# Picked tables in couples: one comparison and one one-hot buffer for two embedding tables in a DLRM tower

## The chip, the cores and the metric

The kernel runs on one core of one Trainium2 chip. Its time is device microseconds (us) of one launch. Before the change three runs gave 159.5, 155.69 and 159.24 us, with a median of 159.24 us. One more execution was recorded by the hardware profiler: it took 156.0 us, of which the span from the first instruction of the program to the last is 154.2 us.

## The reference

For 512 samples the kernel looks up one row of 128 floats in each of 26 embedding tables, adds the sample's `r_bottom_output` as a first feature, takes all 351 dot products of two different features, and sends these with `r_bottom_output` through three layers:

```python
e = jnp.stack([tbl_0[ids[:, 0]], ..., tbl_25[ids[:, 25]]], axis=1)
all_emb = jnp.concatenate([bottom_output[:, None, :], embeddings], axis=1)
gram = jnp.einsum('bfd,bgd->bfg', all_emb, all_emb)
z = gram[:, _TRIU_I, _TRIU_J]
h = jnp.concatenate([z, r_bottom_output], axis=1)
h = jnp.maximum(h @ W_top1 + b_top1, 0.0)
h = jnp.maximum(h @ W_top2 + b_top2, 0.0)
y = h @ W_top3
```

Twelve tables have 1000 rows. The other fourteen have 1250, 12500 or 125000.

## The kernel before

The work has two sources of rows. The twelve tables of 1000 rows are **picked**: a table is loaded whole into SBUF as 128 partitions by 8 places (`RPP`) of 128 floats, and the rows are selected by matmuls against one-hot matrices. The other fourteen tables are **gathered**: an indirect DMA on GpSimd (POOL) brings the 128 rows that one tile of 128 samples needs from one table, 14 gathers for each of four tiles, 56 in all, written by the loop at L168 to L177.

One picked table `i` goes like this. Its 512 ids lie on all partitions in `ids_wide`. VectorE (DVE) writes seven of the eight places of the one-hot buffer `onehot[i % 2]`, one comparison of 128x512 each (L200). ScalarE (ACT) writes the eighth in two steps: `distance` = |id - row| (L256) and relu(1 - 4 * distance) (L269). ACT rounds the table to its high part `table_hi` (L266), DVE subtracts to get the low part `table_lo` (L191), and TensorE (PE) does eight matmuls with the high part (L369) and eight with the low part (L378) into one PSUM bank of `pick_ps`. ACT copies this bank into `features` (`pick_out`, L274). Places are taken in the order 4, 5, 6, 7, 1, 2, 3, 0.

The order of each engine's work is written by hand, and the engines meet at counting semaphores. These matter here. DVE begins the one-hots of table `i` when the picks up to `i - 2` are done (`picked_done`, L198). ACT begins `table_hi` of `i` at the same count (L264), but in its queue that stands behind `pick_out(i - 2)`. PE begins pick `i` when `table_hi` of `i` and `pick_out(i - 2)` are there. SyncE (SP) loads `ids_wide` of `i` and then the table `i` (L141 to L145), and before the load of table `i` it waits until both parts of table `i - 3` exist.

Between the picks stand the **turns**: PE transposes the gathered rows of up to four tables (L391), and DVE or ACT copies them to `features` (L186). `AFTER_PICK` says after which pick each turn comes; turns (t, g) of tile t and group g stand behind picks 2, 3, 4, 5, 7, 8, 9, 10 and 11. A turn holds up the picks behind it until its gathers have landed. The gathers of tiles 2 and 3 write over the rows of tiles 0 and 1, and wait until the same group of that tile is turned (L171).

When all picks are done the **tail** follows: for each tile the products of all feature couples (L404), their transposition on DVE into `grams[t % 2]` (L218, L220), a gathering of bands on ACT (L287), transposes of these (L415) and three layers (L421, L442, L449). In this document the picks are numbered from 0, and "pick 7" is the sixteen matmuls of the eighth picked table.

## Time and profile before

| | |
|---|---|
| runs | 159.5, 155.69, 159.24 us; median 159.24 us |
| profiled execution | 156.0 us, span 154.2 us |
| PE matmul busy | 108.1 us, 70% of the span |
| PE weight load busy | 89.8 us, 58% |
| DVE busy | 66.4 us, 43% |
| ACT busy | 59.2 us, 38% |
| POOL busy | 71.8 us, 47% |
| granted TensorE clock, mean | 0.856 of full speed |

The profiled execution is 3.2 us below the median and 0.3 us above the fastest run. The busy shares are means over stages that differ a lot: DVE is nearly always at work in the first 35 us, and rarely at work in the last 60.

### The profile page before, as it was taken

Reading aid. Unit: us, or ns where it says so; the run is one execution under the profiler, and the core shown is the slowest. Engines: PE = TensorE matmul, PEld = TensorE weight load, DVE = VectorE, ACT = ScalarE, POOL = GpSimd, SP = SyncE. Lnnn points to the kernel's source line nnn. Section 1 sums busy time; section 2 is a strip of 40 time slices with the busy share of each in tenths; the row PEclk is TensorE's granted clock in tenths of the full one; section 3 lists DMA queues with packets and bytes.
Section 4 is the critical chain, followed back from the end, with each engine's and each line's share of the span. In section 5 each row is a group of like instructions: output and inputs, shape, how many; then the busy total and the mean of one; then the engine's idle time right before and its main releaser. Section 6 shows DMA issues by size and latency. Waiting matters only on the chain.

```text
span 154.2 us, 3455 instructions
## 1 busy us (share of the span) xinstructions
PE 108.1 (70%) x1512; PEld 89.8 (58%) x1512; DVE 66.4 (43%) x121; ACT 59.2 (38%) x90; POOL 71.8 (47%) x63
## 2 busy tenths in 40 slices
PE   7598999109996866809429601853799949965994
PEld 7475788008884645608227401742798948855892
DVE  6799999983465439063084003060503005012100
ACT  3576998900455234064080006320304224300612
POOL 1479888997777877787787744000000000000000
PEclk9999999955999786996975865598579999997899
DMA  4999677467126397111112110000000000000000
GB/s 74 347 377 311 227 234 241 165 221 255 51 49 240 96 342 248 51 51 38 51 51 51 51 51 17 21 4 4 4 0 0 4 4 4 0 4 4 0 4 1
DMA packets 7089, 15.23 MB, mean 99 GB/s; under 512 B 1825, under 2 KB 2337, under 8 KB 7074
## 3 DMA queue, kind: packets, MB, share of 16 engines
q1 hardware_dynamic: 5138, 11.07, 20.8%
q0 software_dynamic: 1792, 3.67, 8.6%
q10 hardware_dynamic: 144, 0.26, 0.9%
q8 instruction: 12, 0.20, 0.6%
q14 instruction: 3, 0.02, 0.0%
HBM read 15.00 MB, written 0.00 MB: 97 GB/s over the span
## 4 chain that ended last, share of the span: by engine, by line
PE 35%; another core or an unknown queue 19%; issue 12%; POOL 11%; DMA 8%; ACT 8%; DVE 6%; ACTq 0%; DVEq 0%
POOL rows L174 11%; PE mlp_ps L421 10%; PE prod_ps L404 7%; DMA rows<-in_tbl_dram,ids_all 5%; PE mlp_ps L442 5%; PE mlp_ps L369 4%; PE mlp_ps L378 3%; DVE onehot L200 3%; PE turn_ps L391 3%; DMA ids_all<-in_ids_dram 3%; ACT features L186 2%; ACT table_hi L266 2%; ACT distance L256 1%; PE turn_ps L415 1%
## 5 line engine op out<-in xcount | busy, mean ns | idle before, releaser
L174 POOL DMA_INDIRECT rows<-in_tbl_dram,ids_all x56 | 71.1, 1269 | 23.6 <-issue 16.5
L200 DVE TENSOR_SCALAR onehot<-ids_wide,row_of 128x512 fp32r<-128x512 int32 x84 | 34.5, 485 | 24.4 <-remote 14.9
L369 PE MATMUL mlp_ps<-onehot,table_hi 128*128 128x512 f32 x96 | 31.7, 482 | 15.8 <-DVE onehot L200 13.1
L369 PEld LDWEIGHTS mlp_ps<-onehot,table_hi 128*128 128x128 f32 x96 | 21.6, 236 | 22.2 <-issue 15.5
L274 ACT COPY features<-mlp_ps 128x512 f32<-128x512 f32 x12 | 14.5, 1208 | 46.3 <-remote 28.2
L378 PE MATMUL mlp_ps<-onehot,table_lo 128*128 128x512 f32 x96 | 26.5, 422 | 0.4 <-DVE table_lo L191 0.4
L378 PEld LDWEIGHTS mlp_ps<-onehot,table_lo 128*128 128x128 f32 x96 | 19.7, 208 | 6.1 <-DVE table_lo L191 1.2
L391 PE MATMUL turn_ps<-ident,rows 128*128 128x128 f32 x56 | 10.2, 301 | 15.1 <-ACT features L186 7.2
L186 DVE COPY features<-turn_ps 128x512 f32<-128x512 f32 (+1 forms) x9 | 9.5, 1055 | 24.5 <-PE turn_ps L391 13.2
L404 PE MATMUL prod_ps<-features 128*27 128x27 f32 x1024 | 11.4, 203 | 11.3 <-issue 10.6
L404 PEld LDWEIGHTS prod_ps<-features 128*27 128x27 f32 x1024 | 10.5, 116 | 12.8 <-issue 11.8
L391 PEld LDWEIGHTS turn_ps<-ident,rows 128*128 128x128 f32 x56 | 7.5, 155 | 17.0 <-issue 8.6
L218 DVE STREAM_TRANSPOSE grams<-prod_ps 128x832 f32<-128x832 f32 x4 | 4.2, 1050 | 25.1 <-PE prod_ps L404 25.1
L191 DVE TENSOR_TENSOR table_lo<-table_raw,table_hi 128x1024 fp32r<-128x1024 f32 (+1 forms) x13 | 14.7, 1137 | 0.0
L266 ACT CAST table_hi<-table_raw 128x1024 fp32r<-128x1024 f32 (+1 forms) x12 | 12.1, 1008 | 0.3 <-DMA table_raw<-in_picked_dram 0.2
L421 PE MATMUL mlp_ps<-pairs,w_sb 128*128 128x128 f32 x96 | 11.9, 282 | 0.0
L421 PEld LDWEIGHTS mlp_ps<-pairs,w_sb 128*128 128x128 f32 x96 | 11.6, 200 | 0.0
L287 ACT COPY bands<-grams 128x117 f32<-128x117 f32 (+1 forms) x8 | 3.9, 497 | 16.3 <-DVE grams L218 16.1
L256 ACT ACTIVATE distance<-ids_wide,minus_row 128x512 f32<-128x512 int32 x12 | 8.6, 713 | 2.8 <-DMA ids_wide<-in_picked_ids_dram 2.7
L442 PE MATMUL mlp_ps<-h,w_sb 128*128 128x128 f32 x64 | 9.5, 307 | 0.0
L442 PEld LDWEIGHTS mlp_ps<-h,w_sb 128*128 128x128 f32 x64 | 8.8, 218 | 0.3 <-ACT h L292 0.2
L186 ACT COPY features<-turn_ps 128x512 f32<-128x512 f32 (+1 forms) x7 | 7.4, 1060 | 2.7 <-remote 1.9
(30 smaller groups left out, 52.4 us busy)
## 6 DMA issues: line engine op xcount, KB each, us to landing
table_raw<-in_picked_dram SPq DMA_DIRECT2D x11, 512.0 KB
ids_wide<-in_picked_ids_dram SPq DMA_DIRECT2D x11, 256.0 KB, 3.9
w_sb<-in_W_top_dram SPq DMA_DIRECT2D x4, 256.0 KB
rows<-in_tbl_dram,ids_all POOLq DMA_INDIRECT x56
table_raw<-in_picked_dram SPq DMA_DIRECT2D x2, 256.0 KB, 4.8
w_sb<-in_W_top_dram SPq DMA_DIRECT2D x1, 512.0 KB
ids_wide<-in_picked_ids_dram ACTq DMA_DIRECT2D x1, 256.0 KB, 4.6
bottom_t<-in_bottom_turned_dram SPq DMA_DIRECT2D x1, 256.0 KB
```

Of the source, the lines that this page charges most:

```text
L174: nc.gpsimd.indirect_dma_start(out=rows[t % 2][:, slot - FIRST_G, :], out_offset=None, in_=tables[table], in_offset=bass.IndirectOffsetOnA ...
L186: return engine_copy(dst, turn_ps[n % 2][:, 0:len(slots), :])
L191: return nc.vector.tensor_tensor(table_lo[i % 2][:, begin:end, :], table_raw[i % RAWS][:, begin:end, :], table_hi[i % 2][:, begin:end, :]. ...
L200: nc.vector.tensor_scalar(onehot[i % 2][:, c, :], ids_wide[:, i, :], row_of[:, c:c + 1], None, ALU.is_equal).then_inc(onehot_ready, 1)
L266: nc.scalar.copy(table_hi[i % 2][:, 0:end, :], table_raw[i % RAWS][:, 0:end, :]).then_inc(hi_ready, 1)
L274: nc.scalar.copy(features[:, :, 1 + i], pick_ps[i % 2][:].rearrange("p a b -> p (a b)")).then_inc(picks_ready, 1)
L369: nc.tensor.matmul(acc, table_hi[i % 2][:, c, :], onehot[i % 2][:, c, :], start=(n == 0), stop=False)
L378: last = nc.tensor.matmul(acc, table_lo[i % 2][:, c, :], onehot[i % 2][:, c, :], start=False, stop=(n == RPP - 1))
L391: last = nc.tensor.transpose(turn_ps[n % 2][:, i, :], rows[t % 2][:, slot - FIRST_G, :], ident[:])
L404: last = nc.tensor.matmul(prod_ps[t % 2][32 * s:32 * s + FEATURES, m, 0:FEATURES], features[:, b, :], features[:, b, :], start=True, stop= ...
L421: return nc.tensor.matmul(mlp_ps[n // 2][:, n % 2, :], w1_sb[:, c, 128 * n:128 * n + 128], rhs, start=start, stop=stop, skip_group_check=True)
L442: last = nc.tensor.matmul(mlp_ps[m][:, 2, :], w2_sb[:, c, 128 * m:128 * m + 128], h1[:, c, :], start=(c == 0), stop=(c == 3))
```

## The change

Picked tables go in couples `j` of tables `2j` and `2j + 1`. `ids_wide` becomes two buffers of 2 x 512 ids, loaded alternately, with two semaphores where there were twelve. Each `onehot` buffer holds 8 places x 2 x 512. One DVE comparison covers 1024 ids: six times seven comparisons of 128x1024 stand where twelve times seven of 128x512 stood. ACT's `distance` and its relu also cover 1024 ids, six of each. The table's high and low parts, the sixteen matmuls, `pick_out` and all gathers are as before, one for each table.

The waits shift with it. DVE begins the one-hots of couple `j` when picks up to `2j - 3` are done, and its wait for pick `i - 2` now stands ahead of `table_lo` of each table. ACT writes the eighth place of a couple behind the same count. SP loads the ids of couple `j` ahead of table `2j - 1`, and before that waits until the one-hots of couple `j - 2` are complete. `grams` has one buffer where it had two, so DVE's transposition of tile `t` also waits for ACT's bands of tile `t - 1`.

```diff
-        ids_wide = sb("ids_wide", [128, PICKS, BATCH], i32)
+        ids_wide = [sb(f"ids_wide{i}", [128, 2, BATCH], i32) for i in range(2)]
-        onehot = [sb(f"onehot{i}", [128, RPP, BATCH], f32r) for i in range(2)]
+        onehot = [sb(f"onehot{i}", [128, RPP, 2, BATCH], f32r) for i in range(2)]
-        grams = [sb(f"grams{i}", [128, FEATURES - 1 + BANDS, SLOTS]) for i in range(2)]
+        grams = sb("grams", [128, FEATURES - 1 + BANDS, SLOTS])
@@ sync
-                sp.dma_start(ids_wide[:, i, :], picked_ids[i].partition_broadcast(128)).then_inc(wide_in[i], 16)
+                if i % 2 == 1 and i + 1 < PICKS:
+                    j = (i + 1) // 2
+                    if j >= 2:
+                        sp.wait_ge(onehot_ready, (RPP - ACT_RPP) * (j - 1))
+                        sp.wait_ge(distance_ready, ACT_RPP * (j - 1))
+                    sp.dma_start(ids_wide[j % 2][:], picked_ids[j].partition_broadcast(128)).then_inc(wide_in[j % 2], 16)
@@ vector, pick_operands(i)
-                dve.wait_ge(wide_in[i], 16)
-                if i >= 2:
-                    dve.wait_ge(picked_done, i - 1)
-                for c in PLACES[:-ACT_RPP]:
-                    nc.vector.tensor_scalar(onehot[i % 2][:, c, :], ids_wide[:, i, :], row_of[:, c:c + 1],
-                                            None, ALU.is_equal).then_inc(onehot_ready, 1)
+                if i % 2 == 0:
+                    j = i // 2
+                    dve.wait_ge(wide_in[j % 2], 16 * (j // 2 + 1))
+                    if j >= 2:
+                        dve.wait_ge(picked_done, 2 * (j - 1))
+                    for c in PLACES[:-ACT_RPP]:
+                        nc.vector.tensor_scalar(onehot[j % 2][:, c, :, :], ids_wide[j % 2][:], row_of[:, c:c + 1],
+                                                None, ALU.is_equal).then_inc(onehot_ready, 1)
...
+                if i >= 2:
+                    dve.wait_ge(picked_done, i - 1)
                 low_half(i, 0, HALF if i == 0 else RPP).then_inc(lo_ready, 1)
@@ vector, grams_out(t)
+                if t >= 1:
+                    dve.wait_ge(bands_ready, 2 * t)
@@ scalar, table_high(i): distance and the relu only for even i, on [:, c, :, :]
+                    if j >= 2:
+                        act.wait_ge(picked_done, 2 * (j - 1))
@@ scalar, first load
-            act.dma_start(ids_wide[:, 0, :], picked_ids[0].partition_broadcast(128)).then_inc(wide_in[0], 16)
+            act.dma_start(ids_wide[0][:], picked_ids[0].partition_broadcast(128)).then_inc(wide_in[0], 16)
@@ tensor, pick(i)
-                        pe.wait_ge(onehot_ready, (RPP - ACT_RPP) * i + n + 1)
-                    nc.tensor.matmul(acc, table_hi[i % 2][:, c, :], onehot[i % 2][:, c, :],
+                        pe.wait_ge(onehot_ready, (RPP - ACT_RPP) * (i // 2) + n + 1)
+                    nc.tensor.matmul(acc, table_hi[i % 2][:, c, :], onehot[i // 2 % 2][:, c, i % 2, :],
```

## Rows read from the trace of the kernel before

**Rows 1.** Busy time by stretch: length, then each engine's busy us, clock, DMA, GB/s.

```profile
0.00:34.60 34.60, 24.60 (x108) 19.11 (x108) 31.52 (x64) 23.89 (x31) 25.93 (x20) 0.95 0.73 245
34.60:95.60 61.00, 38.65 (x136) 30.20 (x137) 24.71 (x44) 19.22 (x25) 45.26 (x44) 0.78 0.35 106
95.60:154.20 58.60, 44.81 (x1268) 40.52 (x1268) 10.18 (x13) 16.10 (x35) 0.66 (x1) 0.88 0.02 5
```

**Rows 2.** Timeline, the turn behind pick 4: start, us, engine, what, idle before it.

```profile
25.76 1.99 PE L378 MATMUL mlp_ps<-onehot,table_lo 128*128 128x512 f32 x8
34.62 1.12 PE L391 MATMUL turn_ps<-ident,rows 128*128 128x128 f32 x4 [6.88 <-DMA rows<-in_tbl_dram,ids_all]
```

**Rows 3.** Timeline of POOL, four of its 56 gathers (6th, 12th, 29th, 54th).

```profile
13.03 3.31 POOL L174 DMA_INDIRECT rows<-in_tbl_dram,ids_all  x1 [0.30 <-issue]
...
26.30 6.70 POOL L174 DMA_INDIRECT rows<-in_tbl_dram,ids_all  x1 [0.30 <-issue]
...
56.88 1.18 POOL L174 DMA_INDIRECT rows<-in_tbl_dram,ids_all  x1 [0.31 <-issue]
...
90.18 0.95 POOL L174 DMA_INDIRECT rows<-in_tbl_dram,ids_all  x1 [0.30 <-issue]
```

**Rows 4.** All gathers: ns shortest/median/longest, first and last start in us.

```profile
L174 POOL DMA_INDIRECT rows<-in_tbl_dram,ids_all x56: 940/960/6702, 5.8 to 95.3; - x56
```

**Rows 5.** Waits in total: engine, what, waited for, us, times, longest.

```profile
ACT features L274 <- remote: 28.2, 4, 13.2
```

**Rows 6.** Timeline around pick 10: its last matmuls, its turn, those who wait.

```profile
72.69 2.01 PE L378 MATMUL mlp_ps<-onehot,table_lo 128*128 128x512 f32 x8
74.54 0.38 PE L391 MATMUL turn_ps<-ident,rows 128*128 128x128 f32 x2
...
93.78 1.17 ACT L274 COPY features<-mlp_ps 128x512 f32<-128x512 f32 x1 [13.24 <-remote]
94.06 0.94 POOL L174 DMA_INDIRECT rows<-in_tbl_dram,ids_all  x1 [2.94 <-remote]
```

**Rows 7.** Timeline of one slow round, from pick 7's copy to pick 9's start.

```profile
56.59 1.17 ACT L274 COPY features<-mlp_ps 128x512 f32<-128x512 f32 x1 [5.54 <-PE mlp_ps L378]
56.67 2.86 DVE L200 TENSOR_SCALAR onehot<-ids_wide,row_of 128x512 fp32r<-128x512 int32 x7 [4.65 <-PE mlp_ps L378]
58.14 1.04 ACT L266 CAST table_hi<-table_raw 128x1024 fp32r<-128x1024 f32 x1
59.23 3.47 PE L369 MATMUL mlp_ps<-onehot,table_hi 128*128 128x512 f32 x8 [2.69 <-issue]
```

**Rows 8.** Groups by shape: line, engine, operation, count, busy us, mean ns, idle before.

```profile
L191 DVE TENSOR_TENSOR table_lo<-table_raw,table_hi 128x1024 fp32r<-128x1024 f32 x11 | 13.4, 1221 | 0.0
L191 DVE TENSOR_TENSOR table_lo<-table_raw,table_hi 128x512 fp32r<-128x512 f32 x2 | 1.3, 678 | 0.0
L266 ACT CAST table_hi<-table_raw 128x1024 fp32r<-128x1024 f32 x11 | 11.5, 1044 | 0.2 <-DMA table_raw<-in_picked_dram 0.2
L266 ACT CAST table_hi<-table_raw 128x512 fp32r<-128x512 f32 x1 | 0.6, 622 | 0.1
L256 ACT ACTIVATE distance<-ids_wide,minus_row 128x512 f32<-128x512 int32 x12 | 8.6, 713 | 2.8 <-DMA ids_wide<-in_picked_ids_dram 2.7
L269 ACT ACTIVATE onehot<-distance 128x512 fp32r<-128x512 f32 x12 | 7.6, 634 | 0.0
```

**Rows 9.** Timeline of the start: first comparisons, pick 0's last matmuls.

```profile
5.41 2.86 DVE L200 TENSOR_SCALAR onehot<-ids_wide,row_of 128x512 fp32r<-128x512 int32 x7 [1.02 <-DMA ids_wide<-in_picked_ids_dram]
...
8.93 2.11 PE L378 MATMUL mlp_ps<-onehot,table_lo 128*128 128x512 f32 x8
```

**Rows 10.** Timeline of the tail: bands of tile 0, transposition of tile 1.

```profile
102.81 1.02 ACT L287 COPY bands<-grams 128x117 f32<-128x117 f32 x2 [4.88 <-DVE grams L218]
...
109.54 1.05 DVE L218 STREAM_TRANSPOSE grams<-prod_ps 128x832 f32<-128x832 f32 x1 [5.29 <-PE prod_ps L404]
```

**Rows 11.** Timeline of DVE, the batch of comparisons before the 12th gather's end.

```profile
30.00 2.88 DVE L200 TENSOR_SCALAR onehot<-ids_wide,row_of 128x512 fp32r<-128x512 int32 x7
```

More of the change, by code:

```diff
@@ L65, in dlrm_tower @@
         minus_row = sb("minus_row", [128, RPP])
-        distance = sb("distance", [128, ACT_RPP, BATCH])
+        distance = sb("distance", [128, ACT_RPP, 2, BATCH])
         table_raw = [sb(f"table_raw{i}", [128, RPP, DIM]) for i in range(RAWS)]
@@ L94, in dlrm_tower @@
         ids_in = sem("ids_in")
-        wide_in = [sem(f"wide_in{i}") for i in range(PICKS)]
+        wide_in = [sem(f"wide_in{i}") for i in range(2)]
         first_half_in = sem("first_half_in")
@@ L249, in table_high @@
             def table_high(i):
-                act.wait_ge(wide_in[i], 16)
-                if i >= 1:
-                    act.wait_ge(onehot_act, ACT_RPP * i)
-                for c in range(ACT_RPP):
-                    nc.scalar.activation(distance[:, c, :], ids_wide[:, i, :], ACT.Abs, bias=minus_row[:, c:c + 1]
+                j = i // 2
+                if i % 2 == 0:
+                    act.wait_ge(wide_in[j % 2], 16 * (j // 2 + 1))
+                    if j >= 1:
+                        act.wait_ge(onehot_act, ACT_RPP * j)
+                for c in range(ACT_RPP if i % 2 == 0 else 0):
+                    nc.scalar.activation(distance[:, c, :, :], ids_wide[j % 2][:], ACT.Abs, bias=minus_row[:, c:c + 1]
                                          ).then_inc(distance_ready, 1)
@@ L266, in table_high @@
                 nc.scalar.copy(table_hi[i % 2][:, 0:end, :], table_raw[i % RAWS][:, 0:end, :]).then_inc(hi_ready, 1)
-                for c in range(ACT_RPP):
-                    act.wait_ge(distance_ready, ACT_RPP * i + c + 1)
-                    nc.scalar.activation(onehot[i % 2][:, c, :], distance[:, c, :], ACT.Relu, bias=1.0, scale=-4.0
+                for c in range(ACT_RPP if i % 2 == 0 else 0):
+                    act.wait_ge(distance_ready, ACT_RPP * j + c + 1)
+                    if j >= 2:
+                        act.wait_ge(picked_done, 2 * (j - 1))
+                    nc.scalar.activation(onehot[j % 2][:, c, :, :], distance[:, c, :, :], ACT.Relu, bias=1.0, scale=-4.0
                                          ).then_inc(onehot_act, 1)
@@ L281, in bands_out @@
             def bands_out(t):
-                gram = grams[t % 2][:]
+                gram = grams[:]
                 for half, (begin, end) in enumerate(((0, 1), (1, CHUNKS))):
@@ L377, in pick @@
                         pe.wait_ge(lo_ready, 1)
-                    last = nc.tensor.matmul(acc, table_lo[i % 2][:, c, :], onehot[i % 2][:, c, :],
+                    last = nc.tensor.matmul(acc, table_lo[i % 2][:, c, :], onehot[i // 2 % 2][:, c, i % 2, :],
                                             start=False, stop=(n == RPP - 1))
@@ L508 @@
     ids = _np.asarray(inputs["ids"])
-    arrays["picked_ids"] = _np.ascontiguousarray(ids[:, PICKED].T)
+    arrays["picked_ids"] = _np.ascontiguousarray(ids[:, PICKED].T).reshape(COUPLES, 2, BATCH)
     picked = _np.zeros((PICKS, 128 * RPP, DIM), _np.float32)
```

7 lines of the change are left out of this document (4 added, 3 removed).

## The prediction, made before the changed kernel was built

> **What bounds the kernel now.** I read the share table by stretch first, because one mean for the span hides three stages [rows 1]. In the first 34.6 us DVE is busy 31.5 us: this is the stage in which the change removes work. In the next 61.0 us no engine is busy all the time: PE 38.7, DVE 24.7, ACT 19.2, POOL 45.3. The last 58.6 us is the tail, in which POOL is idle but for one gather and DVE works 10.2 us. So the time is the end of the picks (about 95.6 us) plus the tail (58.6 us) plus 1.8 us that lie outside the span, together 156.0 us. The tail's matmuls are not touched. The question is what moves the 95.6 us.
>
> The timeline of PE names the first limit. Pick 4 ends at 27.75, and the turn behind it starts at 34.62: PE sat still for 6.9 us until gathered rows had landed [rows 2]. The rows are those of the twelfth gather, which POOL began at 26.30 and held for 6.70 us [rows 3]. The reader is to see that DVE's 31.5 us, though nearly all of the stage, are not what PE waits for at its end.
>
> The second limit is odd, and the argument has to live with it. The list of waits has ACT's copy of the picks waiting 28.2 us in four stretches for "remote", that is for an increment whose sender the trace can't name [rows 5]. The code names it: it is PE's own `picked_done`. Pick 10 shows its last matmul ending at 74.70 and its turn at 74.92; ACT starts the copy of pick 10 at 93.78, and POOL, which waits for that turn before its 55th gather, goes on at 94.06 [rows 6]. Two engines see PE's increments 19 us late, at the same time. So PE's increments arrive late in this stage, and no row says why. What the rows do say is when: the lateness is there while POOL issues one gather after another, the median 0.96 us long with 0.30 us between [rows 4], and it is gone 2.6 us after the 54th gather ended at 91.13 [rows 3]. I take it as a working assumption that the late increments belong to this stream of gathers, and that the stage ends soon after POOL runs out of gathers that it may issue.
>
> **The change part by part.** *DVE's comparisons.* Seven of 128x512 take 2.86 us [rows 7], 0.41 us each from start to start. No row shows this operation at 1024. The subtraction on the same engine has both widths, 678 and 1221 ns: 543 ns for 512 more columns, so 135 ns are fixed [rows 8]. With 135 ns fixed, a comparison of 1024 takes 2 x 0.41 - 0.135 = 0.68 us. The bounds are 0.82 us, if nothing is fixed, and 0.62 us, if as much is fixed as on ACT, where a cast goes from 622 to 1044 ns and so has 200 ns fixed [rows 8]. A batch of seven is then 4.8 us (4.3 to 5.7) for two tables, where two batches took 5.7: 0.9 us saved per couple, 5.7 us in all (0 to 8.4). About half lies in the first 34.6 us.
>
> *ACT.* By the slope of the cast (422 ns for 512 columns), `distance` goes from 713 to 1135 ns and the relu from 634 to 1056 ns, six of each instead of twelve [rows 8]. That saves 6 x (0.29 + 0.21) = 3.0 us of ACT in all. In order of work it cuts both ways: `table_hi` of an even table stands behind a `distance` that is 0.42 us longer, that of an odd table comes 0.71 us earlier. ACT's `pick_out`, then `distance`, then `table_hi` lead straight to the next pick but one: 56.59 to 59.18, and PE starts pick 9 at 59.23 [rows 7]. So this chain of 2.6 us gets 0.15 us shorter on the mean of an even and an odd table, 1 us over the seven picks behind 34.6 us. I count it at nothing, because by the assumption above POOL's stream and not this chain sets the end of the stage; if the chain set it, 1 us would be gained.
>
> *The start.* The first ids are 512 KB where they were 256 KB, and the first comparison could start at 5.41 [rows 9]. I allow 0 to 1.4 us for the extra 256 KB and take 0.9, since at the 245 GB/s of the stage [rows 1] 256 KB take 1.1 us and share with the loads of the table. Then the batch ends at 6.3 + 4.8 = 11.1, against 8.27, and pick 0, which ended at 11.04 [rows 9], ends at about 13.7. The second couple follows the low parts of tables 0 and 1, so by then the delay is 1.9 us, and it stays there, since from pick 1 on PE's own work (about 4.1 us for each pick with its turn) is as long as DVE's: 2.4 us of comparisons, 1.2 of subtraction and half a turn's copy. Pick 4 would end at 29.6 instead of 27.75. This costs nothing while the turn behind pick 4 waits for its rows until 34.6; if the rows come early, 1.9 us are lost.
>
> *SP's queue.* The ids of couple 2 wait for couple 0's one-hots, and tables 3 and later are queued behind that wait. Table 3 is held anyway until the low part of table 0 exists, which DVE writes just behind those one-hots, so the wait adds nothing. All table loads of the start move by 1.9 us with the low parts, as do their users.
>
> *Wider gates.* DVE begins couple `j` when pick `2j - 3` is done, one pick earlier than the even table needed before. In the late stage, where DVE waited for increments, that takes DVE's 2.9 us out of the line; but PE started at the end of `table_hi`, before DVE had finished [rows 7], so nothing is gained: ACT's chain is next, and it is as late as before.
>
> *One `grams` buffer.* The added wait is for bands that ACT finished at 103.83, and DVE comes to need the buffer at 109.54 [rows 10]: 5.7 us of cover, and as much again in the later tiles. Cost nothing; queued behind it on DVE is a turn's copy that PE needs 20 us later.
>
> *POOL.* This is where the sum is decided. The gathers themselves are unchanged, but POOL's share of time with DVE at work is not. In DVE's busy stage the 6th gather took 3.31 us and the 12th 6.70 us [rows 3]; the median of all is 0.96 [rows 4]. The 12th ended at 33.00, just behind DVE's batch of 30.00 to 32.88 [rows 11], having seen a batch, a subtraction and a batch go by. Yet the 29th took 1.18 us from 56.88, in the middle of the batch of 56.67 to 59.53 [rows 7]. So a batch holds a gather by chance and until the batch's end. After the change there are six batches of 4.8 us for twelve of 2.86: DVE's busy total shrinks by 5.7 us, each hold is up to 1.9 us longer, and there are half as many. Twelve gathers cost 33.0 - 5.8 = 27.2 us [rows 3, 4] against 15 at the free pace of 0.96 + 0.30 = 1.26; the 12.2 us of holds become anything from 6 (no double hold) to 15 us. I take 11, with DVE's total: a gain of 1 us.
>
> The Trainium skill (SBUF — State Buffer, "Who interferes with whom") states that a DVE instruction in a two-port mode and GpSimd block each other for the whole instruction, the later one waiting in full, and (same page, "SBUF: two separate sides") that descriptors of GpSimd's DMAs can't be written meanwhile. By that rule comparisons of 0.68 us hold each gather longer than those of 0.41, which speaks against the change. The 12th gather agrees (6.70 us), the 29th (1.18 us inside a batch) shows that the hold ends between two instructions at times. By the rule in full the holds would come out at their upper end of 15 us, 3 us more than now, and the sum at 156 + 3 = 159 us; by the rows it is 155.
>
> *Sum.* 156.0 - 1 (POOL) - 0 (ACT's chain) + 0 (start, hidden) + 0 (`grams`) = 155 us on the profiled execution's scale. That execution lay 3.2 us under the median of the three runs, of which one is near it and two are at 159. I expect the changed kernel to scatter alike, and give 155 + 3 = 158 us.
>
> **The rivals.** *Faster: the double hold of the twelfth gather goes.* If the batches leave POOL a gap there, the twelfth gather takes 1.7 us instead of 6.7, so PE's 6.9 us of waiting shrink by 5, less 1.9 if pick 4 ends later; POOL's stream, on which I hang the end of the stage, is 5 us earlier: 156 - 5 = 151, or 154 with the median's offset of 3. For it: DVE has less work and starts couples with more lead. Against: DVE still has 19 us of comparisons for the first four couples without a pause. Chance 0.33.
>
> *Slower: longer holds.* The place is again the first 35 us. A gather that is caught across a batch, two subtractions, a turn's copy and another batch waits 4.8 + 2.4 + 1.2 + 4.8 = 13.2 us instead of 6.7, and the first turns then wait for gathers already behind pick 3. This costs up to 6.5 us: 156 + 6.5 + 3 = 165 us at most, and 163 for two thirds of it. It decides as soon as one gather meets DVE without a pause through two batches. The same ending comes if the comparison at 1024 ran at half the rate (1.2 us each, 8.5 a batch): DVE would take 5.4 us a table and pick 4 would end 5 us later. Chance 0.22 together. The Trainium skill's rule of full blocking (the same section) would lead here too.
>
> *The late increments go.* If they belong not to the gathers but to DVE's and ACT's waits for each table, coupling could end them. Picks 6 to 11 would follow each other in 5 us instead of 10, the products would start when the rows of turn (2, 2) land near 75, and the time would be 156 - 20 = 136 us, 139 on the median's scale. Nothing in the rows points there. Chance 0.05.
>
> *The change does little of what it says* is contained in the forecast: DVE's saving is real but not on the path. Forecast 0.40.
>
> **How the numbers follow.** A run-to-run scatter of 3.8 us in the three runs means that about 2%, or 3.2 us, is what this kernel's measurement can tell from no change. The forecast's own range is 155 to 161. Faster by over 2% (under 156.1) takes the faster rival and the last one, 0.38 together. Slower by over 2% (over 162.4) is the slower rival's but for a hundredth: 0.21. The rest, 0.41, lies within. The range from 150 to 163.5 holds the forecast, the faster rival and the milder half of the slower one, and leaves out 0.05 below and about 0.1 above.
>
> **What would show it.** Comparisons of 128x1024 at 0.68 us from start to start; pick 0's end near 13.7; 42 comparisons with some 29 us busy; ACT's copies of picks 6 to 10 still waiting for "remote"; the 54th gather ending between 85 and 93, and products starting some 4 us later; a tail of 58 to 59 us. The prediction is wrong if the products start far from 2 to 6 us behind POOL's last unheld gather, since then the late increments don't hang on the gathers, and wrong in sign if the twelfth gather's landing moves by more than 5 us either way.

## The result and the profile after

The changed kernel took 148.11 us in the median of four runs (144.81 to 150.53), the kernel before 157.47 us in four runs beside it. The ratio is 0.938, with a 95% interval from 0.928 to 0.948. It is faster by 6%, and 148.11 us lies below the predicted range (150 to 163.5). A ratio here compares only the faster executions of the two kernels, of the kernel before often no more than two or three, which leaves a verdict at the 2% mark open for the experiments up to e15; the medians beside it are of all executions. Its profiled execution took 144.81 us, of which the span is 143.0 us.

By stretch (the same view as [rows 1]; the second stretch ends where the products start at full rate):

```profile
0.00:34.60 34.60, 31.87 (x131) 25.54 (x132) 29.54 (x42) 24.01 (x25) 23.30 (x28) 1.00 0.79 257
34.60:86.00 51.40, 27.29 (x148) 20.62 (x146) 21.07 (x25) 18.69 (x19) 36.78 (x36) 0.79 0.39 120
86.00:143.00 57.00, 43.19 (x1236) 38.80 (x1235) 10.53 (x14) 15.22 (x34) 0.00 (x0) 0.86 0.01 3
```

The tail is 57.0 us where it was 58.6. What went is in front of it: 86.0 us for 95.6. POOL has done 28 pieces of work by 34.6 us where it had done 20; 7 of these are start-up work in both, so 21 gathers stand for 13. None is left for the tail. Why the tail is 1.6 us shorter, no run was made to tell.

The groups of gathers, comparisons and the other parts that the prediction costed:

```profile
L180 POOL DMA_INDIRECT rows<-in_tbl_dram,ids_all x56 | 59.3, 1059 | 21.2 <-issue 16.8 <-DMA ids_all<-in_ids_dram 4.4
L208 DVE TENSOR_SCALAR onehot<-ids_wide,row_of 128x1024 fp32r<-128x1024 int32 x42 | 28.6, 750 | 1.2 <-DMA ids_wide<-in_picked_ids_dram 1.2
...
L197 DVE TENSOR_TENSOR table_lo<-table_raw,table_hi 128x1024 fp32r<-128x1024 f32 x11 | 13.4, 1222 | 4.9 <-issue 4.6
L280 ACT CAST table_hi<-table_raw 128x1024 fp32r<-128x1024 f32 x11 | 11.9, 1078 | 0.9 <-DMA table_raw<-in_picked_dram 0.9
```

POOL's busy time in the gathers is 59.3 us, mean 1059 ns, though no gather was touched. The same line in the trace of before has 11.8 us more:

```profile
L174 POOL DMA_INDIRECT rows<-in_tbl_dram,ids_all x56 | 71.1, 1269 | 23.6 <-issue 16.5 <-DMA ids_all<-in_ids_dram 4.2 <-remote 2.9
```

The timeline of the changed kernel's gathers, from the fourth gather to the twelfth and the last, shows why:

```profile
10.28 1.02 POOL L180 DMA_INDIRECT rows<-in_tbl_dram,ids_all  x1 [0.30 <-issue]
11.60 0.94 POOL L180 DMA_INDIRECT rows<-in_tbl_dram,ids_all  x1 [0.30 <-issue]
...
14.10 1.02 POOL L180 DMA_INDIRECT rows<-in_tbl_dram,ids_all  x1 [0.30 <-issue]
15.42 1.02 POOL L180 DMA_INDIRECT rows<-in_tbl_dram,ids_all  x1 [0.30 <-issue]
16.75 1.02 POOL L180 DMA_INDIRECT rows<-in_tbl_dram,ids_all  x1 [0.30 <-issue]
...
21.26 1.88 POOL L180 DMA_INDIRECT rows<-in_tbl_dram,ids_all  x1 [0.30 <-issue]
...
81.11 0.94 POOL L180 DMA_INDIRECT rows<-in_tbl_dram,ids_all  x1 [0.30 <-issue]
```

The free pace is 0.95 us and 0.30 us between; inside DVE's batches most gathers take 1.02 us, and the longest of the twelve takes 1.88 us. DVE's second batch, seven comparisons in 4.84 us, from 12.78 to 17.62, covers three of them whole and most of a fourth:

```profile
5.61 4.87 DVE L208 TENSOR_SCALAR onehot<-ids_wide,row_of 128x1024 fp32r<-128x1024 int32 x7 [1.23 <-DMA ids_wide<-in_picked_ids_dram]
...
12.78 4.84 DVE L208 TENSOR_SCALAR onehot<-ids_wide,row_of 128x1024 fp32r<-128x1024 int32 x7
```

The twelfth gather ends at 23.14; it ended at 33.00 [rows 3]. The 56th ends at 82.05; before, already the 54th ended at 91.13. On PE, the turn behind pick 4 follows without a wait (before: 6.88 us, [rows 2]), and the picks run on until the last turns. Then comes what was late before too:

```profile
28.33 1.99 PE L394 MATMUL mlp_ps<-onehot,table_lo 128*128 128x512 f32 x8
30.16 0.60 PE L407 MATMUL turn_ps<-ident,rows 128*128 128x128 f32 x4
...
60.83 1.03 PE L407 MATMUL turn_ps<-ident,rows 128*128 128x128 f32 x8
78.14 0.50 PE L420 MATMUL prod_ps<-features 128*27 128x27 f32 x24 [16.27 <-issue]
80.25 0.20 PE L420 MATMUL prod_ps<-features 128*27 128x27 f32 x1 [1.61 <-issue]
83.04 0.20 PE L420 MATMUL prod_ps<-features 128*27 128x27 f32 x1 [2.60 <-issue]
...
86.55 2.50 PE L420 MATMUL prod_ps<-features 128*27 128x27 f32 x190 [0.46 <-issue]
```

PE is through with pick 11 at 61.0 and with the last turns at 61.9. By the code its products wait for ACT's copy of pick 11, and that copy waits for PE's own increment (`picked_done`), seen 16 us late as in [rows 5, 6]:

```profile
76.76 1.17 ACT L290 COPY features<-mlp_ps 128x512 f32<-128x512 f32 x1 [16.24 <-remote]
```

The copy ends at 77.93 and the products begin at 78.14, but then they come singly, and PE is at full rate only 4.5 us after the last gather.

### The profile page after: what moved, and what is told of

Same layout as the page of the kernel before. It is cut to its first block, busy times and chain, and to the rows that moved or that the text cites. A ratio compares the mean times of both kernels' runs of the same rounds, so it can differ in the third digit from the quotient of the medians.

```text
span 143.0 us, 3394 instructions
## 1 busy us (share of the span) xinstructions
PE 102.3 (72%) x1512; PEld 85.0 (59%) x1512; DVE 61.1 (43%) x79; ACT 57.9 (40%) x78; POOL 60.1 (42%) x63
## 4 chain that ended last, share of the span: by engine, by line
PE 64%; issue 25%; DMA 3%; ACT 3%; DVE 2%; DVEq 0%; ACTq 0%
PE mlp_ps L385 18%; PE mlp_ps L394 16%; PE mlp_ps L437 11%; PE prod_ps L420 9%; PE turn_ps L407 5%; DMA ids_wide<-in_picked_ids_dram 3%; PE mlp_ps L458 3%; PE turn_ps L431 2%; DVE grams L230 1%; PE mlp_ps L465 1%; ACT bands L303 1%; ACT features L192 1%; ACT distance L270 1%; DVE features L192 0%; ACT table_hi L274 0%
## 5 line engine op out<-in xcount | busy, mean ns | idle before, releaser
L180 POOL DMA_INDIRECT rows<-in_tbl_dram,ids_all x56 | 59.3, 1059 | 21.2 <-issue 16.8
L420 PE MATMUL prod_ps<-features 128*27 128x27 f32 x1024 | 13.5, 210 | 33.9 <-issue 33.1
L420 PEld LDWEIGHTS prod_ps<-features 128*27 128x27 f32 x1024 | 11.7, 123 | 36.1 <-issue 35.1
L385 PE MATMUL mlp_ps<-onehot,table_hi 128*128 128x512 f32 x96 | 27.6, 429 | 2.7 <-ACT table_hi L274 1.6
L208 DVE TENSOR_SCALAR onehot<-ids_wide,row_of 128x1024 fp32r<-128x1024 int32 x42 | 28.6, 750 | 1.2 <-DMA ids_wide<-in_picked_ids_dram 1.2
L394 PE MATMUL mlp_ps<-onehot,table_lo 128*128 128x512 f32 x96 | 25.0, 404 | 0.4 <-issue 0.4
L385 PEld LDWEIGHTS mlp_ps<-onehot,table_hi 128*128 128x128 f32 x96 | 18.0, 198 | 8.8 <-issue 2.9
L192 ACT COPY features<-turn_ps 128x512 f32<-128x512 f32 (+1 forms) x7 | 7.4, 1059 | 9.4 <-remote 8.9
L458 PE MATMUL mlp_ps<-h,w_sb 128*128 128x128 f32 x64 | 8.3, 280 | 0.0
L308 ACT ACTIVATE h<-mlp_ps 128x256 f32<-128x256 f32 x8 | 3.1, 384 | 12.4 <-PE mlp_ps L437 12.4
L270 ACT ACTIVATE distance<-ids_wide,minus_row 128x1024 f32<-128x1024 int32 x6 | 6.9, 1144 | 2.9 <-DMA ids_wide<-in_picked_ids_dram 2.9
```

Of the source, the lines that this page charges most:

```text
L180: nc.gpsimd.indirect_dma_start(out=rows[t % 2][:, slot - FIRST_G, :], out_offset=None, in_=tables[table], in_offset=bass.IndirectOffsetOnA ...
L192: return engine_copy(dst, turn_ps[n % 2][:, 0:len(slots), :])
L208: nc.vector.tensor_scalar(onehot[j % 2][:, c, :, :], ids_wide[j % 2][:], row_of[:, c:c + 1], None, ALU.is_equal).then_inc(onehot_ready, 1)
L385: nc.tensor.matmul(acc, table_hi[i % 2][:, c, :], onehot[i // 2 % 2][:, c, i % 2, :], start=(n == 0), stop=False)
L394: last = nc.tensor.matmul(acc, table_lo[i % 2][:, c, :], onehot[i // 2 % 2][:, c, i % 2, :], start=False, stop=(n == RPP - 1))
L420: last = nc.tensor.matmul(prod_ps[t % 2][32 * s:32 * s + FEATURES, m, 0:FEATURES], features[:, b, :], features[:, b, :], start=True, stop= ...
```

## The experiments

Two things had to be settled: what let the gathers through (wider comparisons, or the couples' structure and loads), and whether POOL's last gather really sets the end of the stage. Kernels that ran together share a chip, and their ratios are to the kernel before on that chip.

### The comparison's width: e1_narrow, e2_ids_couples

e1 is the changed kernel with each comparison split by table (calls shortened):

```diff
-  tensor_scalar(onehot[j % 2][:, c, :, :], ids_wide[j % 2][:], row_of[:, c:c + 1], None, ALU.is_equal)
+  tensor_scalar(onehot[j % 2][:, c, 0, :], ids_wide[j % 2][:, 0, :], row_of[:, c:c + 1], None, ALU.is_equal)
+  tensor_scalar(onehot[j % 2][:, c, 1, :], ids_wide[j % 2][:, 1, :], row_of[:, c:c + 1], None, ALU.is_equal)
```

> The changed kernel with each comparison of 128x1024 split into two of 128x512, with everything else (couples, buffers, waits, counts) as changed. Theory 1, the width: the comparisons of 1024 let POOL's gathers through where those of 512 held them; then long gathers come back (one of over 3 us among the first twelve), the twelfth ends near 33 us instead of 23, and the time is that of the kernel before, 155 to 159 us. Rival, the structure: what counts is that DVE and ACT get work a table earlier; then the gathers stay short and the time stays at 145 to 150 us, with some 6 us more of DVE busy time hidden.

Measured: 164.55 us beside 161.46, ratio 1.040 (1.023 to 1.057). The holds are back, and worse than the kernel before's; the twelfth gather ends at 40.21, where theory 1 had 33:

```profile
11.53 7.58 POOL L180 DMA_INDIRECT rows<-in_tbl_dram,ids_all  x1 [0.30 <-issue]
...
24.45 4.45 POOL L180 DMA_INDIRECT rows<-in_tbl_dram,ids_all  x1 [0.30 <-issue]
...
31.03 6.67 POOL L180 DMA_INDIRECT rows<-in_tbl_dram,ids_all  x1 [0.30 <-issue]
```

e2 is the kernel before with its ids loaded by couples (the waits of DVE and ACT for the ids follow, not shown):

```diff
-  sp.dma_start(ids_wide[:, i, :], picked_ids[i].partition_broadcast(128)).then_inc(wide_in[i], 16)
+  if i % 2 == 1 and i + 1 < PICKS:
+      sp.dma_start(ids_wide[:, i + 1:i + 3, :], picked_ids[(i + 1) // 2].partition_broadcast(128)
+                   ).then_inc(wide_in[i + 1], 16)
```

> The kernel before, with its ids loaded for two tables at a time: six transfers of 512 KB instead of twelve of 256 KB; comparisons and waits as before. Rival, the transfers: if the smaller number of transfers frees the gathers, the twelfth gather ends near 23 us and the time falls to about 148 us. Theory 1 (the width) and the structure both expect no change: 155 to 159 us, the twelfth gather near 33 us.

Measured: 160.59 us (158.07 to 163.88) beside 161.46: no difference that can be told, and the twelfth gather ends at 33.20. Everything of the change but the width of the comparison loses 2% by the medians, 4% by the ratio; the loads alone do nothing. So the width is the gain. The changed kernel itself did not run beside these two; e7 and e8 below make the same comparison side by side.

### Columns or pattern: e7_flat, e8_wide256

e7 writes the comparison of the changed kernel as one row of 1024 columns; e8 splits it the other way, 256 ids of both tables in each (512 columns in two rows; calls shortened):

```diff
+  # e7
+  tensor_scalar(onehot[j % 2][:, c, :, :].rearrange("p a b -> p (a b)"),
+                ids_wide[j % 2][:].rearrange("p a b -> p (a b)"), row_of[:, c:c + 1], None, ALU.is_equal)
+  # e8, for k in 0, 1
+  tensor_scalar(onehot[j % 2][:, c, :, 256 * k:256 * k + 256],
+                ids_wide[j % 2][:, :, 256 * k:256 * k + 256], row_of[:, c:c + 1], None, ALU.is_equal)
```

> The changed kernel with the same comparisons written over one run of 1024 ids instead of two of 512. If the number of columns of one instruction lets the gathers through, nothing changes: gathers of 1.0 us among DVE's comparisons, 145 to 150 us. Rival: the pattern of two rows does it, and then gathers of over 3 us come back and the time is above 155 us.

> The changed kernel with each comparison split in two, but across: each half covers 256 ids of both tables, so it has 512 columns in two rows. If the number of columns decides, it behaves like the split by table: long gathers, 160 to 166 us. If the pattern of two rows decides, it behaves like the change: 145 to 150 us.

Measured: e7 119.55 us, ratio 0.935 (0.910 to 0.959), longest gather 1.88 us; e8 131.53 us, ratio 1.028 (1.011 to 1.046), longest gather 4.05 us:

```profile
53.39 4.05 POOL L180 DMA_INDIRECT rows<-in_tbl_dram,ids_all  x1 [0.30 <-issue]
```

The number of columns in one instruction decides, not how they lie: e8 is 10% slower than e7, which ran beside it. The times expected for both (145 to 150 and 160 to 166 us) were missed, for a reason of the session: during these runs, on one chip, the kernel before took 129.5 us; in all others its median is 157 to 162 us. The ratio of the change is the same. More of that below.

### Why 512 columns hold a gather: e11_drained, e13_wide_drained

A comparison of 512 columns is 479 ns long in the records, but a batch of seven takes 2.86 us, 0.41 us each: they overlap. Those of 1024 columns overlap as much, 750 ns long and 0.68 us from start to start. And the overlapping narrow ones do not hold every gather: in the first two batches of the kernel before (from 5.41 and 9.40) four gathers took 1.10 to 1.25 us; the 3.31 us of [rows 3] came with the third. In e11, the kernel before, each waits for the signal of the one before it; e13 does the same to the changed kernel.

```diff
-  for c in PLACES[:-ACT_RPP]:
+  for k, c in enumerate(PLACES[:-ACT_RPP]):
+      if k:
+          dve.wait_ge(onehot_ready, (RPP - ACT_RPP) * i + k)      # e13: j for i
```

> The kernel before, in which each comparison of 128x512 also waits for the signal of the one before it, so that they don't overlap: a start to start of about 0.55 us in place of 0.40 and a batch of 3.9 us in place of 2.9. If it is the gapless succession of short comparisons that holds a gather, the gaps let gathers through, no gather takes over 2.5 us, the 12th ends before 28 us and the time falls by 3 to 6% below the kernel before, in spite of the longer batches. If a comparison of 512 columns holds gathers whatever the gap, holds of 3 to 7 us stay, or grow with the batch, and the time is that of the kernel before or 1 to 2% above.

> A version that may beat both kernels: the changed kernel in which each comparison of 128x1024 also waits for the signal of the one before it. If gaps between comparisons let gathers through whatever the width, most gathers take 0.95 us in place of 1.02 to 1.28, POOL's busy time falls from 59 to 54 to 56 us, and the last gather ends 3 to 5 us earlier than in the changed kernel, near 78. Where full-rate products start 4.0 to 4.5 us after the last gather, the time is then 2 to 3% below the changed kernel's. The other theory: a batch of seven takes 5.4 us in place of 4.8, DVE comes later, and PE waits for one-hots, so that the time is the changed kernel's or up to 2% above.

Measured for e11: 150.21 us (145.3 to 151.29) beside 158.07 (154.09 to 162.82, seven runs), 5% less with no overlap of the two; an interval isn't given for it. DVE's batches grew from 2.86 to 4.21 us, the comparisons keep DVE busy for 46.4 us where it was 34.5 (e12), and the kernel is faster. The first batch and the gathers in it:

```profile
5.18 4.21 DVE L202 TENSOR_SCALAR onehot<-ids_wide,row_of 128x512 fp32r<-128x512 int32 x7 [0.79 <-DMA ids_wide<-in_picked_ids_dram]
```

```profile
6.95 0.95 POOL L174 DMA_INDIRECT rows<-in_tbl_dram,ids_all  x1 [0.30 <-issue]
8.20 0.95 POOL L174 DMA_INDIRECT rows<-in_tbl_dram,ids_all  x1 [0.30 <-issue]
```

No gather takes over 1.89 us, and the twelfth ends at 21.99. So comparisons of 512 columns do not hold a gather as such; those 0.41 us from start to start can, those 0.60 us apart did not. Whether it is the overlap or the closer succession that matters, the runs do not part: the 1024-column comparisons overlap too and hold nothing.

Measured for e13: 148.51 us, ratio 0.934 (0.921 to 0.946), against 0.917 (0.909 to 0.926) for the changed kernel beside it. It gains nothing over the changed kernel, and my expectation fails: the gathers keep POOL busy for 64.7 us where I had 54 to 56, and the last one ends at 87.22 where I had 78. In a batch a gather takes 1.27 us, 1.58 us from start to start:

```profile
16.02 1.27 POOL L180 DMA_INDIRECT rows<-in_tbl_dram,ids_all  x1 [0.30 <-issue]
17.60 1.28 POOL L180 DMA_INDIRECT rows<-in_tbl_dram,ids_all  x1 [0.30 <-issue]
```

Its comparisons start every 5.53 / 7 = 0.79 us, and 1.58 is two of these. In the changed kernel gathers start every 1.33 us (15.42, 16.75) with comparisons every 0.67 to 0.69 us: two again. In e11 two comparisons take 1.20 us, less than a gather's own 1.25, and nothing is held. The rows fit a GpSimd that gets through one gather for every two comparisons, so that slower comparisons, once nothing is held, only cost. This was not tested otherwise, and it does not explain the holds: two comparisons 0.41 us apart take 0.82 us, less than 1.25. Why gathers are held there stays open.

### Early or late holds: e9_narrow_early, e10_narrow_late, e12_before

e9 splits as e1 does for couples 0 to 2 (`if j < 3`), e10 for couples 3 to 5 (`if j >= 3`); e12 is the kernel before.

> The changed kernel with the comparisons of couples 0 to 2 split into two of 128x512, and those of couples 3 to 5 left at 1024 columns. If the gain is that the first 12 gathers land earlier for the first turns, nearly all of it goes: the 12th gather ends after 30 us, the turn behind pick 4 waits again, and the time is 3 to 5% above the changed kernel's. If it is the end of POOL's whole stream (late holds count as much as early ones), about half of the loss of the fully split kernel comes here, some 3 to 4 us.

> The mirror: couples 0 to 2 at 1024 columns, couples 3 to 5 split. By the first theory (early gathers feed the turns) this costs nothing, since the picks run ahead with rows to spare: within 1% of the changed kernel, if TensorE's signals are prompt on this chip. By the second theory it costs the other half, 3 to 4 us, and the last gather ends 3 to 5 us later than in the changed kernel.

> The kernel before as it is, for a trace on this chip beside the other three. Holds of 3 to 7 us by the batches of 512-column comparisons are expected on any chip. If TensorE's signals are prompt here, the span is near 128 us; if they are late, as in the first traces, it is 154 to 160 us. Both theories say the same of this run: it only tells which kind of chip the other three ran on.

Measured: e9 152.62 us, ratio 0.982 (0.964 to 1.000); e10 152.17 us, 0.967 (0.938 to 0.997); e12 155.93 us. Against the changed kernel's ratios on other chips (0.938 and 0.917) each half costs 3 to 7%; as the changed kernel did not run beside them and both intervals are wide, the halves can't be told apart. Late holds cost about as much as early ones, where the theory of the early gathers had them cost nothing: the last gather ends at 89.06 in e9 and 90.53 in e10. They make PE wait for rows too, three times in e10's trace (of the execution of 153.87 us), the longest before the turn that precedes the products:

```profile
67.12 1.12 PE L413 MATMUL turn_ps<-ident,rows 128*128 128x128 f32 x4 [4.33 <-DMA rows<-in_tbl_dram,ids_all]
```

But the products then still crawl until behind the last gather, so at this pace of the gathers it is the end of POOL's stream that counts. How the stage ends in e12:

```profile
68.53 0.66 PE L391 MATMUL turn_ps<-ident,rows 128*128 128x128 f32 x4 [3.17 <-DMA rows<-in_tbl_dram,ids_all]
69.12 0.69 PE L404 MATMUL prod_ps<-features 128*27 128x27 f32 x37
70.32 0.24 PE L404 MATMUL prod_ps<-features 128*27 128x27 f32 x1 [0.52 <-issue]
71.02 0.20 PE L404 MATMUL prod_ps<-features 128*27 128x27 f32 x1 [0.45 <-issue]
...
91.31 0.20 PE L404 MATMUL prod_ps<-features 128*27 128x27 f32 x1 [2.60 <-issue]
...
96.21 2.02 PE L404 MATMUL prod_ps<-features 128*27 128x27 f32 x152 [0.46 <-issue]
```

The picks are done at 64.9 and the products begin at 69.12, but after 37 of them they come singly, at steps of 0.70 us or a multiple, "issue" before each: PE waits for nothing that the trace shows. Full rate returns 4.3 us after the last gather. So in all traces of this kind (times read from the timelines, the products' first long group being full rate):

| us | last gather ends | products at full rate | span |
|---|---|---|---|
| after | 82.05 | 86.55 | 143.0 |
| e13 | 87.22 | 91.49 | 145.8 |
| e9 | 89.06 | 93.43 | 150.4 |
| e10 | 90.53 | 94.96 | 152.1 |
| e12 (before) | 91.92 | 96.21 | 154.1 |
| e2 | 98.75 | 102.88 | 158.4 |
| e1 | 102.46 | 106.50 | 162.8 |

4.0 to 4.5 us in every row. e12 also shows how much the holds differ between executions of one kernel: its twelfth gather ends at 28.94 and its longest takes 3.61 us, where the first trace of before had 33.00 and 6.70; the spans are 154.1 and 154.2 us all the same. In the first trace of before, in e11 and in e14 PE's increments were late during the picks instead, the picks ended only at 83 to 91, and the products' full rate came 0.4 to 2.8 us after the last gather. So e14's expectation (4.0 to 4.5 us behind the last gather, at 82 to 84 us) missed: POOL, too, waited for PE's increments there, and its last gather ended at 86.21.

### Fewer gathers: e3_before_half, e4_after_half

The kernels before and after with the gathers of tiles 2 and 3 left out (their turns read the rows of tiles 0 and 1; two waits change with it, not shown):

```diff
-  for t in range(TILES):
+  for t in range(2):
```

> The kernel before, without the gathers of tiles 2 and 3 (28 of 56 left; tiles 2 and 3 use the rows of tiles 0 and 1). Theory 2, the gathers make PE's increments late and their end sets the end of the stage: POOL is done near 52 us, from some 3 us later on no increment is late, picks follow each other in 5 us, and the products start near 75 us instead of 96: about 135 us. Rival, PE's increments are late for a reason of PE's own work: the late ones stay up to the last pick, the products start near 95 us and the time stays over 150 us.

> The changed kernel, without the gathers of tiles 2 and 3 (28 of 56 left; tiles 2 and 3 use the rows of tiles 0 and 1). Theory 2: POOL is done near 42 us, the last picks end near 60 us as now, but the products start right then, at 62 us instead of 86, so about 121 us. Rival (PE's own work makes them late): the copy of pick 11 still waits until about 76 us and the time stays near 145 us.

Measured: e3 128.21 us, ratio 0.813 (0.805 to 0.822), no wait for "remote" in its trace, products at 68.43, just behind the picks. e4 136.6 us (129.52 to 139.22) where 121 was expected; no ratio is given. The first bears the assumption out: without POOL's late gathers the stage ends with the picks. The second was a surprise. Its 28 gathers run unheld, one each 1.25 us, and are done at 42.26; by then PE had stood for 9.1 us. The trace is of an execution of 139.22 us and another took 129.52 us, so how much of this all four had isn't known:

```profile
26.22 0.38 PE L405 MATMUL turn_ps<-ident,rows 128*128 128x128 f32 x2
27.43 0.27 PE L405 MATMUL turn_ps<-ident,rows 128*128 128x128 f32 x1 [0.83 <-issue]
28.16 0.32 PE L405 MATMUL turn_ps<-ident,rows 128*128 128x128 f32 x1 [0.46 <-issue]
37.59 3.78 PE L383 MATMUL mlp_ps<-onehot,table_hi 128*128 128x512 f32 x8 [9.11 <-issue]
```

The picks' own matmuls come singly here between 43.65 and 45.05, and are at full rate from 45.75, 3.5 us after the last gather. The 33 us from there to the products at 78.72 are picks at 4 us each.

Where the holds are gone the early stretch may suffer: gathers in close succession seem to do harm that held ones do not. e14's trace, of an execution of 143.71 us in which no gather took over 2.0 us, has such a stretch as well (ACT's copy at 47.50 waited 14.45 us for "remote"). That is a theory on their pace.

### The pace of the gathers: e5 and e6, e14, e15 to e18

A memset on POOL and a wait for it stand ahead of each gather of tiles 1 to 3 of the changed kernel:

```diff
+  if t >= 1:                                            # e18: t >= 2
+      nc.gpsimd.memset(pause[:], 0.0).then_inc(paused, 1)
+      paused_times += 1
+      pool.wait_ge(paused, paused_times)
```

`pause` is 128x512 in e5, e15 and e18, 128x1024 in e6, 128x128 in e16 and 128x256 in e17.

> The changed kernel with a pause on POOL before each gather of tiles 1 to 3: a memset of 128x512 into a scratch tile, and a wait for it, some 0.6 us more per gather. Theory 2a, the density of the gathers makes PE's increments late: with one gather in about 1.9 us none is late, the products start near 62 us instead of 86, the tail is held a little by the gathers of tile 3 (the last near 105 us), and the time is 120 to 128 us. Rival 2b, gathers at any density do it until the last one is done: the gathers end near 105 us and the time is about 165 us.

> As the last one, with a memset of 128x1024, some 1.1 us more per gather, so one gather in about 2.4 us. Theory 2a: no late increments either, but tile 3's rows come near 122 us, so 132 to 140 us. Rival 2b: the end of the stage moves with the last gather, about 185 us. If 0.6 us is too short a pause and 1.1 is not, this one is faster than the last.

Measured, in the session of e7 and e8: e5 130.48 us, ratio 1.018 (1.003 to 1.033), e6 142.35 us, 1.116 (1.098 to 1.135). They told nothing of the theory, because no engine waited for "remote" there: e7's products start at full rate at 60.20, right behind the picks, though its gathers go on until 82.92.

```profile
59.61 0.66 PE L408 MATMUL turn_ps<-ident,rows 128*128 128x128 f32 x4 [0.53 <-DMA rows<-in_tbl_dram,ids_all]
60.20 3.46 PE L421 MATMUL prod_ps<-features 128*27 128x27 f32 x219
```

So e5 ran once more in a session in which the kernel before took 162.29 us, beside the changed kernel (e14). The memsets are not free for DVE: its comparisons are 889 ns long on the mean in e5 and 1042 ns in e6, for 748 in e7.

> The changed kernel as it is, beside the other two on this chip. On a chip where the kernel before takes 155 to 162 us, full-rate products should start 4.0 to 4.5 us after the last gather (82 to 84 us), and the time be 146 to 150 us; on one where the kernel before takes 129 us they start right behind the picks, near 60 us, and the time is 119 to 122 us. The ratio to the kernel before is 0.93 to 0.95 on both.

> The kernel e5 once more: a memset on POOL ahead of each gather of tiles 1 to 3, so that gathers come about every 3 us in place of 1.25 and the last one ends near 101 us. Where the kernel before takes 129 us it gives 130 us again and tells nothing new. Where it takes 155 to 162 us: if PE is served slowly as long as any gather is still to come, full-rate products start 4 us after the last gather, near 105, and the time is 162 to 165 us. If it is the close succession of gathers that does it, PE runs as on the other chip and the time is 129 to 135 us, below the changed kernel's 148.

Measured: e14 145.15 us, ratio 0.917 (0.909 to 0.926); e15 135.72 us, 0.856 (0.846 to 0.866). The last gather ends at 102.21, 16 us later than in e14, and the kernel is 6.5% faster: it is the pace. Gathers start 1.91 us apart among DVE's comparisons (not 3, as I had expected) and 1.76 us apart behind them, where the products are. PE gets some 42 products done in each of these intervals:

```profile
73.71 0.32 PE L427 MATMUL prod_ps<-features 128*27 128x27 f32 x5 [0.46 <-issue]
74.46 0.70 PE L427 MATMUL prod_ps<-features 128*27 128x27 f32 x37 [0.43 <-issue]
75.48 0.30 PE L427 MATMUL prod_ps<-features 128*27 128x27 f32 x4 [0.32 <-issue]
76.22 0.70 PE L427 MATMUL prod_ps<-features 128*27 128x27 f32 x38 [0.44 <-issue]
```

```profile
73.10 0.95 POOL L187 DMA_INDIRECT rows<-in_tbl_dram,ids_all  x1 [0.27 <-POOL pause L184]
74.86 0.95 POOL L187 DMA_INDIRECT rows<-in_tbl_dram,ids_all  x1 [0.27 <-POOL pause L184]
```

The last three ask how long the gap must be, and where.

> As e15 with the smallest pause: a memset of 128x128 and a wait ahead of each gather of tiles 1 to 3, so that gathers start about 1.5 us apart in place of 1.25 (and 1.91 in e15). If TensorE is freed in proportion to the gap between two gathers, products still come a few at a time until 4 us after the last gather (near 88), and the time is 142 to 148 us. If any gap behind a gather is enough, PE is served as in e15 and the rows come earlier than there: 128 to 133 us.

> The pause between the two: 128x256, gathers about 1.65 us apart, the last one ending near 93. By the first theory the time is between those of e16 and e15, or the best of the three if e15 pauses longer than it needs (133 to 140 us); by the second it is that of e16 plus up to 2 us.

> The pause of e15 (128x512) only ahead of the gathers of tiles 2 and 3; tiles 0 and 1 come at full pace, as in the changed kernel, until about 42 us. If it is the products' stretch behind the picks that must be free of a close succession, this is as good as e15 or better, 130 to 135 us. If the close succession in the first 40 us already sets off the late signals, as in e4, where half the gathers at full pace gave 137 us, the time is 137 to 145 us, with a stretch of over 8 us in which PE starts nothing.

Measured, beside 157.45 us for the kernel before: e16 146.6 us, ratio 0.929 (0.922 to 0.937); e17 141.08 us, 0.897 (0.890 to 0.905); e18 144.78 us, 0.903 (0.893 to 0.914). e12, e14 and e15 ran on other chips than these three.

| gathers start apart, in the products' stretch | products done per interval | ratio to before |
|---|---|---|
| 1.25 us (e12, e14) | 1 or 2 (e12) | 0.917 (e14) |
| 1.44 us (e16) | some 10 | 0.929 |
| 1.55 us (e17) | some 20 | 0.897 |
| 1.76 us (e15) | some 42 | 0.856 |

For the products the effect grows with the dose: the longer the gap, the more of them pass. From 1.25 to 1.76 us they grow by some 41 for 0.51 us, 80 for each us added (47 and 67 for the two smaller pauses); PE's long groups run at 76 (190 in 2.50 us, above) to 109 (239 in 2.19 us, e15's at 103.61) for each us. So, by this estimate, PE works at most at its full rate in the time that the pause adds, and hardly at all in the rest. The time follows only from 1.55 us on: at 1.44 us it is no better than without a pause (0.929 and 0.917). e18 has the long gap only from tile 2 on, and in its trace, of an execution of 146.54 us (the four took 141.27 to 147.4), PE stands for 8.4 us in the early stretch, as e4's did:

```profile
35.98 3.63 PE L392 MATMUL mlp_ps<-onehot,table_hi 128*128 128x512 f32 x8 [8.41 <-issue]
```

With its ratio of 0.903 against e15's 0.856 on another chip, this speaks for the early gathers' pace counting too. Of the versions with all gathers e15 is the fastest where PE is held, and e5, the same kernel, is 9% slower than e7 where it is not. The changed kernel (e7, in its other spelling) beats the kernel before by the same 6 to 8% in both kinds of session.

## Why the prediction was wrong

*Where it failed.* In the part on POOL: "the 12.2 us of holds become anything from 6 (no double hold) to 15 us. I take 11, with DVE's total: a gain of 1 us." Twelve gathers started at 5.97 and ended at 23.14, so 17.2 us against 15 at the free pace: 2.2 us of holds were left, not 11, and not within the bounds either. Over all 56 gathers POOL was busy for 59.3 us instead of 71.1 (69.4 in e12). I had scaled the holds with DVE's busy total, as if a batch were one block. The 29th gather, 1.18 us inside a batch, already said that it isn't, and I read it as chance. e1 and e8 show that the width lets the gathers through, e11 that comparisons of the old width do the same when each waits for the one before it. The 12.2 us were themselves one execution's: e12 had 8.2.

*The size of it.* POOL's stream ended 9.1 us earlier (82.05 for the 54th gather's 91.13, with two more gathers done), the second stretch 9.6 us earlier and the tail took 1.6 us less: 95.6 + 58.6 = 154.2 became 143.0. With 10 us in place of 1 us the prediction's own sum gives 146 on the profiled scale, 149 on the median's; measured were 144.81 and 148.11.

*What held.* The working assumption, that the stage ends soon after POOL runs out of gathers, held in the ten traces with all gathers, no pause and PE held (0.4 to 4.5 us), and e3 and e15 show that the gathers are its cause. They are not enough by themselves: in the session of e7 the same gathers held up nothing. The sign that I had set for it came too: full-rate products 4.5 us behind the last gather. "ACT's copies of picks 6 to 10 still waiting for 'remote'" held in kind only: in this trace two copies wait some 2 us (at 36.45 and 40.83), and the lateness sits at the last pick and the products. Comparisons: 0.68 us predicted, 4.84 / 7 = 0.69 measured; batch 4.8 and 4.84; busy 29 and 28.6. `distance` took 1144 ns where 1135 was predicted. Pick 0 ended at 14.49, not 13.7, and pick 4 at 30.32, not 29.6; the turn behind it had its rows, so its start was the picks' own. The single `grams` buffer cost nothing that shows.

*Signs that failed.* The twelfth gather's landing moved by 9.9 us, which I had named as the sign of being wrong in direction (over 5 us either way). The 54th gather ended at 79.55, outside 85 to 93, and the tail took 57.0 us, not 58 to 59.

*The rivals.* The faster one was the mechanism that happened ("the batches leave POOL a gap there"), but priced at one gather's hold, 5 us, when all holds went. It had 0.33 and its 154 us was 6 us too high. The slower one had it the wrong way round: it said longer batches mean longer holds. The Trainium skill's rule of full blocking (SBUF — State Buffer, "Who interferes with whom") speaks of one instruction that blocks the other engine for its whole length, not of a batch. That holds would grow with the batch, to 15 us, was my own step from it, and 1.02 us gathers inside 4.84 us batches refute that step. Steps of two comparisons from gather to gather would go with a block of one instruction at a time; a hold of 7.58 us beside comparisons of 0.48 us (e1) would not by itself, and no run here shows what makes it last.

*An excluded rival.* "The late increments go" was set against DVE's and ACT's waits. They shrink with the pace of the gathers, for 135.72 us in e15. That this is near the 139 us that I gave this rival is luck: it is another cause and another kernel.

## What to carry to other kernels

When GpSimd issues gathers beside a train of short VectorE instructions, look at single gathers inside single batches: if they last until the batch's end, make the instructions wider, or let each wait for the one before it, though VectorE then takes longer. Before costing anything, ask whether the end of GpSimd's stream, or its pace, sets another engine's stage; if products come singly with "issue" before them while gathers run, a slower stream can be the faster kernel, but measure it in more than one session. And price a faster rival with all the places its mechanism acts on, not with the one that the trace happens to name.

## What the hardware showed that I had not expected

- Comparisons of 512 columns at 0.41 us each hold a gather for up to 7.58 us; at 0.60 us each (e11), or 1024 columns at 0.69 us (the changed kernel, e7 and e14), the longest gather takes 2.0 us.
- While gathers start every 1.25 us, PE's products come singly, 0.70 us or a multiple apart, and increments are seen up to 19 us late; with 1.76 us from gather to gather some 42 products pass in each interval. The Trainium skill (Runtime: NRT & Kernel Launch, "Instruction fetch mechanics") says that an engine's instructions come by a DMA queue of its own in blocks of 256, and that the cost of a new block is mostly hidden. The single steps are finer than such a block, and no run here ties them to it.
- This comes and goes on one chip: the kernel before took 129.5 us in one session (products at 60 us in e7) and 157.45 us in another. What differs between sessions stays open, and so does the way by which gathers hold PE up.
